# A graph layer with 212,500 edges on one core: SyncE fetches 44 rows in four quads in place of 32

## The reference

```
h = max(layernorm(x), 0);  xp = h @ lin1                      # per node
C = 0.5 * (cos(edge_weight * pi / 10) + 1)
W = (ssp(edge_attr @ mlp_w1 + b1) @ mlp_w2 + b2) * C[:, None]   # per edge, ssp = softplus - log 2
msg = xp[src] * W;  agg = segment_sum(msg, dst)
out = x + (ssp(agg @ lin2_w + lin2_b) @ lin_w + lin_b)
```

## Time and profile before

| | us |
|---|---|
| median of 3 runs | 2026.22 (2023.22 to 2027.63) |
| the profiled execution, its own time | 2022.45 |
| its span, from the first to the last instruction | 2020.7 |
| GpSimd busy | 1517.5 (75%) |
| TensorE busy | 1341.8 (66%) |
| VectorE busy | 1048.1 (52%) |
| ScalarE busy | 792.7 (39%) |

### The profile page before, as it was taken

How to read it: one execution, slowest core, us unless ns; L and a number is a source line. 1 busy time by engine, 2 the same in 40 slices (tenths; PEclk the granted TensorE clock), 3 DMA queues, 4 the chain that set the end, 5 groups by cost and what they waited for, 6 DMA issues and landing times.

```text
span 2020.7 us, 48993 instructions
## 1 busy us (share of the span) xinstructions
PE 1341.8 (66%) x12880; PEld 1108.7 (55%) x12881; DVE 1048.1 (52%) x3153; ACT 792.7 (39%) x925; POOL 1517.5 (75%) x1611
## 2 busy tenths in 40 slices
PE   5577667776776777676666666666666666666666
PEld 5465556655555556555555555555555555555454
DVE  8664655555545555555544444444544444445454
ACT  5764333333434443433343333333333334333332
POOL 7777777777777777777777777777777777777775
PEclk9887888888888878888787888778877878887887
DMA  9633343333343344334333233333333333333322
GB/s 320 247 94 92 89 97 88 98 98 92 92 99 97 88 97 99 87 93 102 87 88 97 77 97 90 84 98 81 92 94 80 98 86 88 97 88 87 96 76 51
DMA packets 114579, 202.33 MB, mean 100 GB/s; under 512 B 36409, under 2 KB 69917, under 8 KB 114173
## 3 DMA queue, kind: packets, MB, share of 16 engines
q0 software_dynamic: 51392, 105.35, 21.6%
q1 hardware_dynamic: 55228, 91.86, 14.7%
q10 hardware_dynamic: 7680, 1.98, 0.7%
HBM read 186.25 MB, written 12.80 MB: 99 GB/s over the span
## 4 chain that ended last, share of the span: by engine, by line
POOL 38%; ACTq 19%; issue 18%; ACT 16%; PE 4%; DVE 3%; DMA 1%; DVEq 0%; SPq 0%; POOLq 0%
POOL XG L460 38%; ACTq L576 17%; ACT TB L593 5%; ACT TB L587 4%; ACT TB L590 4%; ACTq L565 1%; PE PW L878 1%; ACT XG L482 1%; DMA XG<-xp_scratch,IX 1%; PE PA L897 1%; DVE XG L776 1%; DVE TB L651 1%; DVE SCR L630 1%; PE PX L824 1%; PE PX L862 0%
## 5 line engine op out<-in xcount | busy, mean ns | idle before, releaser
L460 POOL DMA_INDIRECT XG<-xp_scratch,IX x1542 | 1455.6, 944 | 470.6 <-issue 463.0
L776 DVE SCALAR_TENSOR_TENSOR XG<-PW,CC,XG 128x128 f32<-128x128 f32 x1602 | 453.1, 344 | 435.3 <-DMA XG<-xp_scratch,IX 399.6
L587 ACT ACTIVATE TB<-PX 128x1024 f32<-128x1024 f32 x208 | 212.8, 1023 | 1039.8 <-PE PX L862 532.9
L875 PE MATMUL PW<-BPB,ones 128*128 128x512 bf16 x415 | 183.7, 443 | 563.3 <-DVE XG L776 558.8
L878 PEld LDWEIGHTS PW<-W,TB 128*128 128x128 f32 x3314 | 545.9, 234 | 20.0
L878 PE MATMUL PW<-W,TB 128*128 128x128 f32 x3314 | 548.9, 320 | 0.0
L731 DVE SCALAR_TENSOR_TENSOR TB<-PX,TB 128x1024 f32<-128x1024 f32 x208 | 254.2, 1222 | 347.1 <-ACT TB L593 336.5
L875 PEld LDWEIGHTS PW<-BPB,ones 128*128 128x128 bf16 x415 | 41.2, 99 | 674.2 <-issue 670.2
L897 PE MATMUL PA<-OH,XG 128*64 128x64 f32 x6408 | 296.1, 259 | 0.0
L897 PEld LDWEIGHTS PA<-OH,XG 128*64 128x64 f32 x6408 | 265.4, 171 | 31.3 <-issue 18.4
L862 PE MATMUL PX<-AT,W 51*128 51x256 f32 x1662 | 258.2, 432 | 2.6 <-ACT XG L482 2.6
(11 more groups left out here) (107 smaller groups left out, 538.1 us busy)
## 6 DMA issues: line engine op xcount, KB each, us to landing
HA<-xp_scratch ACTq DMA_DIRECT2D x3840, 0.5 KB
AT<-attr_b SPq DMA_DIRECT2D x104, 512.0 KB
HT<-xp_scratch SPq DMA_DIRECT2D x3092, 0.5 KB
XG<-xp_scratch,IX POOLq DMA_INDIRECT x1542, 2.7
AG<-zero SPq DMA_DIRECT2D x1, 6400.0 KB, 21.6
xp_scratch<-XG SPq DMA_DIRECT2D x24, 256.0 KB
XR<-x SPq DMA_DIRECT2D x24, 256.0 KB
out<-XR SPq DMA_DIRECT2D x24, 256.0 KB, 3.8
```

Source lines behind the costliest of these rows:

```text
L460: e.indirect_dma_start(XG[q % XG_N][0:p, k * D:(k + 1) * D], None, xp, bass.IndirectOffsetOnAxis(ap=IX[0:p, t0 + k:t0 + k + 1], axis=0)).t ...
L587: e.activation(T, PXP[pair % 2][:, :], ACT.Abs).then_inc(s_ab, 1)
L776: ins = e.scalar_tensor_tensor(out=G, in0=weights(q)[0:p, k * D:(k + 1) * D], scalar=CC[0:p, t0 + k:t0 + k + 1], in1=G, op0=ALU.mult, op1= ...
L875: e.matmul(P[0:p, 0:n * D], ones[:, 0:p], BP[0][:, 0:n * D], start=True, stop=False, skip_group_check=True)
```

## The change

SyncE's share of the rows grows from 32 to 44 a turn. The numbers of a turn now stand in one row of the table `SI`, which becomes 101 rows (`TURNS`) of 44, and are loaded in two pieces, 24 and 20. A piece may now go over the end of a tile, so the wait for a tile's buffer stands inside the list of rows. `HQ` gives tile j to quad 18 + 4 ceil(128 (j + 1) / 44), that is 30, 42, 54 and so on to 402, and a last tile of 20 rows to quad 414: 34 tiles and 4244 rows. GpSimd leaves out the first tile of these quads. ScalarE's rows, the number of buffers (three) and all other work stay.

```diff
-ROWS = 32
-NH = (NCH - 3 - 2) * ROWS // TILE
-HQ = {18 + (j + 1) * TILE * CHQ // ROWS: j for j in range(NH) if 18 + (j + 1) * TILE * CHQ // ROWS < NQ - 2}
+ROWS = 44
+TURNS = NCH - 3
+HQ = {18 + -(-(j + 1) * TILE // ROWS) * CHQ: j for j in range((TURNS - 2) * ROWS // TILE)}
+HQ = {q: j for q, j in HQ.items() if q < NQ - 2}
 HQ[NQ - 2] = len(HQ)
 HAND = sorted(HQ)
 NH = len(HAND)
...
-        SI = sb("SI", [NH, TILE], i32)
+        SI = sb("SI", [TURNS, ROWS], i32)
...
-            def fetch(a, b):
-                n = a
-                while n < b:
-                    j, p = n // TILE, n % TILE
-                    m = min(8 - n % 8, b - n)
-                    if p == 0 and j >= HT_N:
-                        e.wait_ge(s_sc, HAND[j - HT_N] + 1)
+            def fetch(turn):
+
+                for h, m in ((0, 24), (24, ROWS - 24)):
+                    n0 = turn * ROWS + h
+                    if n0 >= END:
+                        return
                     _, at = nc.values_load_multi_w_load_instructions(
-                        SI[j:j + 1, p:p + m], engines=[mybir.EngineType.SP], min_val=0, max_val=ROW * (NODES - 1),
+                        SI[turn:turn + 1, h:h + m], engines=[mybir.EngineType.SP], min_val=0, max_val=ROW * (NODES - 1),
                     skip_runtime_bounds_check_because="src holds node numbers, which are below NODES")
-                    for i, v in enumerate(at):
-                        e.dma_start(HT[j % HT_N][p + i:p + i + 1, :].bitcast(u8), row(v)).then_inc(s_r[j % HT_N], 16)
-                    n += m
+                    for n, v in zip(range(n0, END), at):
+                        j, p = n // TILE, n % TILE
+                        if p == 0 and j >= HT_N:
+                            e.wait_ge(s_sc, HAND[j - HT_N] + 1)
+                        e.dma_start(HT[j % HT_N][p:p + 1, :].bitcast(u8), row(v)).then_inc(s_r[j % HT_N], 16)
...
-                fetch(min(END, (k - AT_N) * ROWS), min(END, (k - AT_N + 1) * ROWS))
+                fetch(k - AT_N)
...
-        "src_h": _np.ascontiguousarray(tiles(g["src"]).T[[quad(q)[0] for q in HAND]]),
+        "src_h": turns(tiles(g["src"]).T[[quad(q)[0] for q in HAND]], TURNS, ROWS),
```

## The result

The changed kernel takes 2061.84 us (median of 4 runs, 2061.01 to 2063.05) beside 2024.72 us for the kernel before on the same chip: a ratio of 1.0185, with a 95% interval of 1.0169 to 1.0201. It is 37 us slower, where 11 us less had been forecast. The profiled execution has a span of 2059.2 us.

The account below looks back on a forecast made before the run. The prediction took GpSimd's gathers to bound the edge loop; nine fewer save 11.2 us and all other terms cost nothing, so the median falls from 2026.22 to 2015.0 us, with a range of 2011 to 2028.

Parts of the forecast that it names:

- The reading of the kernel before: Whole edge loop: GpSimd's gathers bound it at 1.249 us each; consumers run beside it, SyncE third with some slack.
- Part (1): GpSimd's line: 1533 gathers in place of 1542, nine by 1.249 us, saves 11.2 us, all on the bounding line.
- Part (2): SyncE's turn: twelve more rows at 0.33 us and two larger loads lengthen it from 14.5 to 18.1 to 18.3 us.
- part (5): Table scaling before the loop, HBM-to-SBUF transfers of the rows and completion of hand tiles: each costs nothing.
- 1896: SyncE's queue: predicted issue time in us of chunk 99 (quads 396 to 399), with 18.15 us a turn and 28 for stores.
- Part (3): Chunk 99 on SyncE: may be issued as late as about 1905 us, is due at 1896, a reserve of 9 us.
- Part (4): SyncE's wait for a hand tile's buffer, three buffers, tiles changing every 2.9 turns: counted at nothing.
- SyncE becomes the bound: Rival on SyncE's queue: turns past break-even at 18.37 us make the kernel slower, 2040 us at 18.5; chance 0.15.
- Gathers: Sign on GpSimd: 1533 gathers of 944 ns with 0.30 us between, the last starting near 1998 us.
- VectorE's waits for gathered rows: Sign on VectorE: these waits shrink from some 400 us to less than 200 and begin after 1400 us.
- Turns of 18.1 to 18.2: Sign on SyncE: its turns, without stores, are 18.1 to 18.2 us apart.
- SyncE's waits gone: Sign on SyncE: hardly any wait for TensorE until the last turns.

Follow-up runs that it names:

- 14 rows: Against the changed kernel, ScalarE fetches 14 rows in place of 20 in two quads, SyncE keeps 44 a turn: 2022.97 us, ratio 0.9999.
- half rows: Against the changed kernel, rows of 256 bytes in place of 512 in SyncE's and ScalarE's transfers: 2052.26 us, ratio 1.0142.

## Why the prediction was wrong

**The reading of the kernel before** held: GpSimd is the bound without holes, the consumers are a second line, SyncE the third. **Part (1)**, nine gathers by 1.249 us, held: the last one starts 10.5 us earlier by the earlier trace rows.

**Part (2), SyncE's turn, is the step that failed**, in one of its terms: the price of a row. The loads came out within the bounds (a median of 1.606 us over loads of 24 and of 20; together some 3.15, the upper bound), and the first four turns, 18.22 us, lie in the range of 18.1 to 18.3. But the 0.33 us of a row is only what SyncE's queue needs to issue it. I took it as its whole price, and in part (5) I wrote that the rows' transfers cost nothing. SyncE's rows and ScalarE's share something that passes one row in 0.229 us on average. With 84 rows in four quads that is 19.23 us, whatever SyncE's own work is. The three kernels with SyncE's same 44 rows show the split: with 40 rows of ScalarE in four quads chunk 99 comes at 1972.7, with 28 at 1912.5, with none at 1903.5. So my 1896 was 8 to 17 us short for SyncE's own work, and the shared rate added the other 60 to 69.

The backlog can be read from the traces. If ScalarE's 512-byte packets are put beside its issues, in order, a row waits from the end of its issue to the start of its packet for 0.72 us with 14 rows and 0.98 us in the kernel before; it waits 9.3 us in the changed kernel, 11.7 with 40 rows, 9.2 with 42, 13.4 without stores and 9.0 with half rows (medians from 300 to 1850 us). In the changed kernel it is 1.1 us before 200 us and 10.2 from 300 to 600. The page shows the same in the time of ScalarE's packets (queue, packets, MB, share of 16 engines), in the kernel before, the changed one and the one with 14 rows; per packet the third is about a third of the second:

```profile
q10 hardware_dynamic: 7680, 1.98, 0.7%
```

```profile
q10 hardware_dynamic: 7680, 1.98, 1.3%
```

```profile
q10 hardware_dynamic: 5376, 1.39, 0.3%
```

The kernel before was already near that rate. In its first half four quads take 17.06 us for 72 rows, 0.237 us each, and from 300 to 600 us its rows wait 1.7 us. I had this pace and the count of rows in my hands and never divided one by the other over both queues. The short bursts did not warn: in the first 160 us of the changed kernel's row fetching both queues issue at full speed, and only when they have done so for long are rows held up. What waits then is seen in the reads of `x`, which stand behind them: they land after 14.7 us.

**Part (3)**, the deadline of chunk 99, had the right mechanism and the wrong size. I let SyncE be as late as 1905. With 1912.5 and 1542 gathers nothing was lost. With 42 rows the chunk came at 1932.9 and the span was 2024.4, against the 2010.7 that eight gathers fewer would give: 13.7 us lost, so the deadline was near 1919. Two of its terms were off. From activation 198 to 207 the consumers need 5.79 us each and not 8.53, so they can work off some 36 us and not 10.9:

```profile
1986.33 1.02 ACT L589 ACTIVATE TB<-PX 128x1024 f32<-128x1024 f32 x1 [6.26 <-PE PX L864]
...
2038.47 1.02 ACT L589 ACTIVATE TB<-PX 128x1024 f32<-128x1024 f32 x1 [1.64 <-PE PX L864]
```

Against that, chunk 99 is behind the backlog: activation 198 starts 13.7 us after its issue, where I counted 4.8. Together the two move the limit by some 16 us, and with the values of the kernel with 42 rows (6.42 and 13.4) by some 10, beside the 14 that its span shows. This error went the other way and softened the first. Why the consumers are that fast at the end no run isolates; ScalarE issues its last row at 1974.3.

**Part (4)**, the wait for a tile's buffer at no cost, held: no wait on line 421 is among SyncE's waits. In the kernel with the chunks on ScalarE's queue, where SyncE runs ahead at first, it does wait there, 32.9 us in all before 500 us.

**The rivals.** What came is the slower one, SyncE becomes the bound, with its break-even at 18.37 us a turn. I gave it 0.15, because it needed 0.35 us more than computed. It got 0.8 us, by a cause that I had not named. Its slope held roughly: from 42 to 44 rows the turn grows by 0.446 us, which is 42.8 us over 96 turns, and the spans differ by 34.8. The page's rate of 200 ns for each register in the Trainium skill ("Runtime: NRT & Kernel Launch", section "Instruction fetch mechanics") is not what made it: the loads of 20 and 24 numbers take 1.45 us at least and 1.606 at the median.

**The signs.** Gathers: right. VectorE's waits for gathered rows were to shrink to less than 200 us; there are none, as the consumers never meet GpSimd. Turns of 18.1 to 18.2: right for the first 70 us only. SyncE's waits gone: right. Activations 8.5 us apart to 700 us: wrong, they are 9.3 apart from 200 to 890, as the changed kernel shows at line 589, 75 starts from 200.3 to 890.2:

```profile
L589 ACT ACTIVATE TB<-PX x75: 1003/1023/1024, 200.3 to 890.2; 128x1024 f32<-128x1024 f32 x75
```

**What stays open** is where rows share the 0.229 us. It is not SyncE's queue, as ScalarE's rows decide it; it is not bytes; and it lies behind the issue and ahead of the packets, as the waits of 9 to 13 us there show. Rows do not pass evenly: in the kernel without stores a quarter of the row packets start within 0.03 us of the one before and a twentieth more than 1 us after it, although some 27 of ScalarE's rows wait (the median at an issue). No two neighbours of them start less than 0.021 us apart, whichever queue they are from, as if all passed one place. Whether that is a generator of transfers that both queues use, or one engine that all transfers of a single row fall to, no run here tells. Nor did any run vary GpSimd's gathers, which go on at the same 1.249 us beside the rows in every kernel and may set the rate with them. That six rows more or less on one queue can be traded for others on the other was shown for ScalarE's side only.

## What to carry to other kernels

When work is moved off a full engine onto queues with time to spare, count how many transfers all queues together issue in the period of the loop, and compare that with the highest sustained rate that a trace has shown; the issue time of one queue is not its price. Here 80 rows in four quads gave 8 us, 82 gave nothing and 84 cost 37 us: close to such a rate the optimum has a cliff beside it, so try one step less before the whole. A landing time that grows for a transfer that was not changed is a sign of the backlog: a store of 512 nodes takes 3.8 us in the kernel before and 12.8 in the changed one. It is not a sign of lost time, as the fastest complete kernel here, with 40 rows, has 16.1.

## What the runs showed of the hardware

Transfers of one row, issued by SyncE and ScalarE together, pass at 0.227 to 0.229 us each over long stretches, in five kernels, with 256 bytes as with 512 (0.228). Bursts go faster than that: rows of one queue follow each other every 0.33 us, and both queues issue at once without a hold in the first turns. Behind that rate a row of ScalarE waits 9 to 13 us between its issue and its packet, where it otherwise waits 0.7 to 1.0.

A load of numbers from SBUF takes 0.449 us for one and 0.792 for eight on SyncE, and 1.606 at the median for 20 and 24, so each further number adds about 0.05. The Trainium skill ("DMA: Bandwidth & Descriptors", section "Latency and other measured facts") gives `tensor_load` a floor of some 600 ns. The 449 ns of the earlier trace rows are below that, and the measurement decides.
